# Attention scores from three products a tile, queries paired two steps ahead, one copy moved from ScalarE to GpSimd

## What is computed

```
Q = layernorm(x) @ Wq.T + bq      K = ctx @ Wk.T + bk      V = ctx @ Wv.T + bv
scores = Q K^T * SCALE / temperature        (per head: 32 terms a score)
x = x + softmax(scores) V @ Wo.T + bo
```

## Time and profile before

| what | value |
|---|---|
| median of three runs | 1847.13 us |
| profiled execution: its own time | 1846.3 us |
| profiled execution: span of core 0 | 1844.5 us |
| mean granted TensorE clock | 0.985 |
| `attend` in the profile | about 164 to 936 us |
| `rest` in the profile | from about 936 us |

### The profile page before, as it was taken

One profiled execution on the slowest core, in us unless ns is written; L12 is line 12 of the kernel. 1 busy time (PEld: TensorE's weight loads), 2 busy tenths in 40 slices (PEclk: granted clock), 3 DMA queues, 4 the chain that ended last, 5 costly groups with the idle time before them and its releaser, 6 DMA issues. The chain is left out here.

```text
span 1844.5 us, 30104 instructions
## 1 busy us (share of the span) xinstructions
PE 1766.0 (96%) x9338; PEld 1327.2 (72%) x9418; DVE 1562.1 (85%) x3587; ACT 1232.8 (67%) x3374; POOL 969.4 (53%) x1079
## 2 busy tenths in 40 slices
PE   8897799999999999999879999889999999999997
PEld 7676688888888888888744444357677777777775
DVE  6865889999999999988769888888888988888885
ACT  4574999999999999999733333265665655665543
POOL 2333466666666666666610000056776776676664
PEclk9998999999999999999989999999999999999999
DMA  8565334544454445433379999154455455454311
GB/s 303 194 225 151 81 103 119 133 122 115 118 133 122 115 116 135 119 94 92 81 227 380 401 396 390 74 206 157 162 173 176 160 172 180 155 173 162 129 58 40
DMA packets 143278, 306.35 MB, mean 166 GB/s; under 512 B 44432, under 2 KB 52624, under 8 KB 125456
## 3 DMA queue, kind: packets, MB, share of 16 engines
q1 hardware_dynamic: 142976, 304.17, 51.4%
q10 hardware_dynamic: 144, 0.26, 0.0%
HBM read 164.90 MB, written 105.91 MB: 147 GB/s over the span
## 5 line engine op out<-in xcount | busy, mean ns | idle before, releaser
L1261 POOL TENSOR_TENSOR a_pr<-a_pr,a_rcp 128x512 f32<-128x512 f32 x256 | 266.4, 1041 | 281.4 <-DVE a_rcp L1107 281.2
L1017 ACT ACTIVATE a_pr<-a_s,a_nmax 128x128 f32<-128x128 f32 x1024 | 364.0, 380 | 15.8 <-DVE a_nmax L1100 14.2
L1507 PE MATMUL f_pair<-f_room,w 128*128 128x512 bf16 x999 | 224.7, 382 | 2.6 <-ACT f_room L1618 1.3
L1017 ACT ACTIVATION_READ_ACCUMULATOR a_pr<-a_s,a_nmax 128x1 f32 x1024 | 224.0, 219 | 0.0
L1926 POOL TENSOR_TENSOR f_rs<-f_rs,f_half 128x1 f32<-128x1 f32 x128 | 121.2, 947 | 179.6 <-DVE f_rs L1773 179.6
L1727 DVE CUSTOM_DVE_ANT_0 f_hf<-f_pair,nb,sh 128x512 f32<-128x512 f32 x244 | 172.7, 748 | 29.4 <-PE f_pair L1507 29.2
L1100 DVE TENSOR_REDUCE a_nmax<-a_s 128x4 f32<-128x512 f32 x256 | 172.3, 673 | 15.4 <-PE a_s L907 15.2
L1656 ACT ACTIVATE f_room<-f_ring,f_off,f_rs 128x511 f32<-128x511 f32 (+1 forms) x128 | 104.4, 816 | 120.2 <-POOL f_off L1932 120.2
L1115 DVE TENSOR_TENSOR a_pTl<-a_pt,a_pTh 128x512 fp32r<-128x512 f32 x256 | 168.5, 679 | 19.1 <-ACT a_pTh L1029 18.5
L1507 PEld LDWEIGHTS f_pair<-f_room,w 128*128 128x128 bf16 x1024 | 99.5, 98 | 116.4 <-issue 3.2
L919 PE MATMUL a_pt<-ident,a_pr 128*128 128x128 f32 x1024 | 155.4, 274 | 3.9 <-POOL a_pr L1261 3.8
(11 more groups left out here) (381 smaller groups left out, 5071.5 us busy)
## 6 DMA issues: line engine op xcount, KB each, us to landing
hidden<-f_hf SPq DMA_DIRECT2D x57, 1024.0 KB, 8.5
f_hf<-hidden SPq DMA_DIRECT2D x57, 1024.0 KB, 4.8
xb<-x SPq DMA_DIRECT2D x16, 1024.0 KB, 5.7
ctxh<-bqreph SPq DMA_DIRECT2D x128, 128.0 KB, 2.3
ctxh<-bqrepl SPq DMA_DIRECT2D x128, 128.0 KB, 2.4
a_xr<-x SPq DMA_DIRECT2D x64, 256.0 KB, 3.8
x<-a_xr SPq DMA_DIRECT2D x64, 256.0 KB, 2.6
f_ring<-x SPq DMA_DIRECT2D x64, 256.0 KB, 3.2
```

Of the source, the lines that this page charges most:

```text
L1017: last = e.activation(pr[:, t, j, :], s_bank[t][:, j * P:j * P + P], ACT.Exp, bias=nmax[kk % 2][:, t, j:j + 1], accum_out=sums[kk % 2][:, ...
L1261: e.tensor_tensor(p, p, rcp[kk % 2][:, t, :].unsqueeze(2).to_broadcast([P, 4, KEYS]), ALU.mult).then_inc(*e_pn)
L1507: last = e.matmul(h_bank[(PAIRS * u + i) % 3][:, q, :], w1[:, k, f * P:f * P + P], xT[u % 2][:, k, :], start=k == 0, stop=k == KC - 1)
```

## The change

1. `scores`: a tile takes three products of 256 columns, not four. The 12 products of 32 rows that four heads need (three per head) are laid as blocks of 32 rows into three planes of 128 rows; plane 0 adds into columns 0 to 255, plane 2 into 256 to 511, plane 1 into 128 to 383.
2. Keys and queries are laid out for that: `KEY_BLOCKS` (six DMAs a quarter, as before) and `QUERY_BLOCKS` (eight DMAs a step, 384 rows of 512 values, where there were four with 256 rows). The keys of two of the four quarters of the first batch are loaded in `prepare`, those of the others in the first two steps of `attend`.
3. QUERY is 2, XT 6, LOAD 11: queries and all before them one step earlier. `paired` waits for the last scores of step kk, since it overwrites the tile they read. The order of TensorE, ScalarE and VectorE changes in step 0; from step 1 on it is as before, except that the first half of `queries` is behind `scores` 0 in steps 1 to 4 too.
4. `chi` leaves ScalarE. GpSimd's `clo` now first waits for `vsum`, copies `cs` to the high half and waits for its own copy.
5. `vals` takes three DMAs a quarter, not eight. GpSimd clears the values' tile with one memset, not four.

```diff
-KEY_ROWS = ((0, 0, 0), (0, 0, 64), (1, 1, 0))
+KEY_BLOCKS = ((0, 0, 0, 3, 0, 0), (1, 0, 1, 3, 0, P), (2, 1, 0, 2, 0, 0), (2, 0, 3, 1, 2, P), (3, 1, 2, 2, 1, P),
+              (3, 0, 0, 1, 0, 0))
+QUERY_BLOCKS = (((0, 0, 0, 64), (2, 0, 64, 64), (1, 64, 32, 64), (0, 64, 0, 32), (2, 96, 96, 32)),
+                ((1, 0, 32, 64), (0, 96, 0, 32), (2, 64, 96, 32)))
+KEYS_HERE = 2
...
-        LOAD, LN_A, LN_B, NORM, XT, QUERY = 10, 8, 7, 6, 5, 1
+        LOAD, LN_A, LN_B, NORM, XT, QUERY = 11, 9, 8, 7, 6, 2
...
                 e_exp.wait_ge(e, 4 * (u - 1) + (2, 1, 4, 3)[t])
-                for i in range(2):
-                    for n, x in enumerate(kt):
-                        last = e.matmul(s_bank[t][:, 256 * i:256 * i + 256], qs[kk % 2][:, i, t * P:t * P + P], x[:, c, i, :],
-                                        start=n == 0, stop=n == 1)
+                for plane, at in ((0, 0), (2, 2 * P), (1, P)):
+                    last = e.matmul(s_bank[t][:, at:at + 2 * P], qs[kk % 2][plane][:, t * P:t * P + P], kt[c][:, plane, :],
+                                    start=plane == 0, stop=plane == 1)
                 last.then_inc(*e_s)
...
-            def chi(b, kk):
-                o = kk - VALUE
-                if not there(b, o):
-                    return
-                u, c, g = b * TPB + o, o % 4, o // 4
-                e_vs.wait_ge(e, 2 * u + 1)
-                e.activation(cT[g % 2][0][:, c, :], cs[:], ACT.Copy).then_inc(*e_chi)
...
                 phi(b, kk, 2)
                 phi(b, kk, 3)
                 if opening:
-                    xhi(b, 0)
-                chi(b, kk)
+                    xhi(b, kk)
                 exp(b, kk, 3)
...
-            for c in range(KC):
-                last = e.memset(f32(vp[:, c, :, :]), 0.0)
-            last.then_inc(*e_const)
+            e.memset(f32(vp_room[:]), 0.0).then_inc(*e_const)
...
                 c, g = o % 4, o // 4
+                e_vs.wait_ge(e, 2 * (b * TPB + o) + 1)
+                e.tensor_copy(cT[g % 2][0][:, c, :], cs[:]).then_inc(*e_chi)
                 e_chi.wait_ge(e, b * TPB + o)
                 e.tensor_tensor(cT[g % 2][1][:, c, :], cs[:], f32(cT[g % 2][0][:, c, :]), ALU.subtract).then_inc(*e_clo)
...
-                if not there(b, o):
-                    return
+                if not there(b, o) or first(b) and o < ASKED:
+                    return
+
+                e_s.wait_ge(e, 4 * (b * TPB + o - 2) + 3)
                 for h, e_half in ((0, e_qhi), (1, e_qlo)):
-                    if not first(b) or o >= ASKED:
-                        e_half.wait_ge(e, b * TPB + o - ASKED)
-                    for i in range(2):
-                        e.dma_start(f32(qs[o % 2][64 * h:64 * h + 64, i, :]), f32(qT[h])[64 * i:64 * i + 64, :])\
+                    e_half.wait_ge(e, b * TPB + o - ASKED)
+                    for plane, to, at, n in QUERY_BLOCKS[h]:
+                        e.dma_start(f32(qs[o % 2][plane][to:to + n, :]), f32(qT[h])[at:at + n, :])\
                             .then_inc(e_qs[o % 2].sem, 16)
```

More of the change, by code:

```diff
@@ L819, in attend @@
         e_const, e_b = ev("const"), ev("bias", 16)
-        e_kt, e_v = ([ev(f"{n}{c}", unit) for c in range(KC)] for n, unit in (("keys", 96), ("values", 128)))
+        e_kt, e_v = ([ev(f"{n}{c}", unit) for c in range(KC)] for n, unit in (("keys", 96), ("values", 48)))
         e_qs = scr["e_qs"]
@@ L884, in xt @@
                     e_qlo.wait_ge(e, 1 - ASKED)
-                elif again:
-                    e_xlo.wait_ge(e, o - 1 - TURNED)
-                elif there(b, kk + QUERY):
+                elif there(b, kk + QUERY) and not (first(b) and kk < 0):
                     e_qlo.wait_ge(e, b * TPB + kk + QUERY - ASKED)
@@ L986, in step @@
                 pt(b, kk, 1)
-                if not opening:
+                if opening:
+                    xt(b, -1)
+                else:
                     queries(b, kk, 1)
                 scores(b, kk, 2)
+                if opening:
+                    queries(b, kk, 0)
+                    queries(b, kk, 1)
                 values(b, kk)
-                if opening:
-                    xt(b, -1)
                 pt(b, kk, 2)
@@ L995, in step @@
                 pt(b, kk, 3)
-                if not first(b) or kk >= 0:
-                    xt(b, kk, again=opening)
+                xt(b, kk)
                 out(b, kk)
@@ L1073, in step @@
                 if opening:
-                    xhi(b, -1)
-                elif not first(b) or kk > 0:
+                    qhi(b, kk)
+                else:
                     xhi(b, kk)
@@ L1212, in step @@
                 opening = first(b) and kk == 0
-                if opening:
+                if first(b) and kk < 0:
                     qlo(b, kk)
+                    return
                 rc(b, kk - 1, 3)
                 smax(b, kk, 0)
+                if opening:
+                    xlo(b, -2)
                 plo(b, kk, 0)
@@ L1220, in step @@
                 rc(b, kk, 0)
+                if opening:
+                    xlo(b, -1)
                 plo(b, kk, 1)
@@ L1227, in step @@
                 smax(b, kk, 2)
-                if not opening:
-                    qlo(b, kk)
+                qlo(b, kk)
                 vsum(b, kk, 0)
@@ L1232, in step @@
                 vsum(b, kk, 1)
-                if opening:
-                    xlo(b, -1)
-                elif not first(b) or kk > 0:
+                if not opening:
                     xlo(b, kk)
@@ L1381, in step @@
             def step(b, kk):
-                if not first(b) or kk >= 0:
-                    paired(b, kk)
+                paired(b, kk)
                 load(b, kk)
```

92 lines of the change are left out of this document (55 added, 37 removed).

## The result

| what | before | after |
|---|---|---|
| median of the runs | 1847.41 us | 1874.58 us |
| lowest and highest | 1845.5 to 1848.08 | 1874.15 to 1876.47 |
| ratio, 95% interval | | 1.0155 [1.0141, 1.0169] |
| span of the profiled execution | 1844.5 us | 1872.3 us |
| second `vlow` of step 0 and of step 63 | 189.56, 917.06 | 201.34, 946.41 |

`vlow` is ScalarE's reading of the attended values. The start of the second one of a step is called its zero. The change makes the kernel 1.55% slower, 27 us. The forecast was 1867 us (1855 to 1888) and slower with 0.86. The time lies in the range, 7.6 us above the forecast.

What follows compares the result with a forecast made beforehand. TensorE's queue was taken as the bound, by 0.25 us over the GpSimd loop. 57 x 11.89 + 6 x 10.85 = 742.8 against 727.5 us (+15.3), with 2.4 + 2 opening +19.7: 1866.0 profiled, 1867 us median, range 1855 to 1888.

Steps and rivals of the forecast that it cites:

- The loop: From zero over `xhi`, `xlo`, `rc` 2, `prob` 2, `clo`, `prob` 3, `pt` to next zero: 11.22 of 11.47 us, slack 0.25.
- What the prediction says of `rc` 3: In `attend`, VectorE's own queue holds `rc` 3, so ScalarE's saved 0.67 us is off the loop and worth nothing.
- The copy: In `clo` on GpSimd, between `prob` 2 and `prob` 3: 0.61 us plus 0.08 semaphore wait, 0.69 uncovered.
- The rival with a price of 1.04: GpSimd's copy costs 1.04 us like a two-input operation, adding 25 us: 1892 us; chance 0.10.
- The body by port speed: Copy on GpSimd at 1.03 cycles an element, 1.2 GHz: estimated 0.44 us for 512 elements, total 1857 us.
- Three products for four: In `scores`: four tiles save 0.48 us of TensorE's queue a step; the loop gains only one tile's 0.12.
- The step: Steady step of `attend`: loop 11.84 us, plus 0.05 for the step with normalisations, 11.89 us.
- The range of 1858 to 1876: The forecast's own range, from the opening's bounds and a copy on GpSimd between 0.525 and 0.75 us.
- The opening: Start of `attend`: four more SP loads, 2.4 us, plus step 0's full `queries` and `xt`, 2 us (bounds 0 and 4).
- SP's queue: Eight query issues take 4.8 us, `qhi` keeps 1.4 us slack; rival: SP late in 16 steps, 1883 us, chance 0.05.
- The last six steps and `rest`: Last six steps of `attend` have no `xt`: 10.85 us each; `rest` is untouched.
- nobody waits for those within a step: On SP behind `paired`, loads of x, store, reload, values and keys, some 11 issues, 6.6 us, hold nobody up.

Runs made afterwards that it cites:

- before_copy_pool: Kernel before with only the copy of the attended values' high half moved from ScalarE to GpSimd; 1868.95 us, ratio 1.0128.
- experiment 3: Changed kernel with the copy still on GpSimd, but copy and `clo` moved behind `prob` 3; 1853.1 us, ratio 1.0047.
- experiment 9: On experiment 6: step 0's queries behind `pt` slot 3, `clo` behind `prob` 3, `x1_stats` behind `rc` 3 and next `smax` 0; 1884.09 us, 1.0215.
- experiment 6: Also `stats_first`: changed kernel with the copy back on ScalarE and step 0's statistics and `rstd` ahead of all else in `attend`; 1838.9 us, 0.9967.
- experiment 7: Changed kernel, copy on GpSimd, with step 0's statistics and `rstd` ahead of all else in `attend`; 1864.3 us, ratio 1.0113.

## Why the prediction was right, and where it was off

**The loop: right, for more work in it.** "Nothing in between has slack", said of `xhi` to `prob` 3, and a slack of 0.25 us at `pt`, were what decided. In `before_copy_pool`, 0.69 us of new work on an engine with a third of its time idle cost 0.40 us a step, where 0.69 less 0.25 is 0.44. That is the step of the prediction that carries the sign, and the experiment that shows it changes nothing but the copy. What the prediction says of `rc` 3, that VectorE's queue holds it, is half of it: ScalarE's `exp` 3 ends 0.03 us ahead of it (506.38 and 506.41), so ScalarE's list was on this loop as much as GpSimd's. That didn't matter to the forecast, since the copy made GpSimd's way longer than the others (`prob` 3 ends at 7.45 us and not at 6.83). It is why less work on GpSimd gained nothing in experiments 3 and 9.

**The copy: right.** Forecast 0.61 with 0.08 for its own semaphore; measured 0.612 on average (0.609 to 0.619 over all 64), and 528.34 to 529.03 is 0.69. The rival with a price of 1.04 fell. The body by port speed that the prediction took from the Trainium skill, "GPSIMD Engine Reference", section 3.1 (an estimate of 0.44 us) is 0.17 too short for the instruction. But the growth from the cast of 128 columns to the one of 512 is 0.612 - 0.289 = 0.323 us for 384 columns, 0.84 ns a column, and 1.03 cycles at 1.2 GHz are 0.86. So the page's rule fits what each column adds, and what it leaves out is the fixed part, by an estimate from these two rows 0.18 us, with 0.08 for the wait behind it. The two casts differ in what they write (bf16 and fp32r), so this rests on the type making no difference, which no run here shows.

**Three products for four: right in its mechanism.** Forecast: four tiles save 0.48 us of TensorE's queue, one tile's 0.12 shortens the loop, and the rest is lost in the wait. Measured: 11.90 against 11.80 for the 0.12 (`before_copy_pool` and the changed kernel), and the idle time of 0.68 + 0.05 at `pt` for a forecast of 0.8. TensorE's busy share came out at 95.5% where "about 93%" was expected, since the view counts a product to its modelled end and not to the next one's start: 0.81 of 11.80 us is 7%.

**The step: right, and better than its parts.** 678.0 us in 57 steps are 11.89, the number of the prediction. A plain step of a window in the middle is 11.80 (forecast 11.84), one with the normalisations 11.96 to 12.02 (forecast 12.06). Steps 1 and 3 at 12.85 and 12.63, and one of 12.83 behind a late load of x, make up the difference. So a part of that agreement is chance. The range of 1858 to 1876 that the prediction calls its own would be 1860 to 1877 by the bounds that it names for it; the stated range of 1855 to 1888 doesn't hang on it.

**The opening: the term that was mis-sized.** The step of the prediction is "Step 0 now also holds a full `queries` and an `xt` (...) Bounds 0 and 4 us, I take 2." It measured 9.3, above the upper bound. SP's part, 4 x 0.6 = 2.4, was right: the eight issues take 5.0 us (160.79 to 165.80) where four took 2.5 (160.90 to 163.35). That the starts agree to the tenth is chance, since TensorE's first product lies between 165.96 and 167.37 in the ten profiles with eight loads, and at 164.07 and 164.94 in the two with four. For step 0 I had counted what TensorE gets more of. I had not asked which piece of the layer norm falls on it: with LN_B at 8 in place of 7, two more statistics and the `rstd` of the group land in step 0, where VectorE is late as it is and GpSimd's list puts `rstd` ahead of `prob` 2. Experiments 6 and 7 show that piece: 7.1 us, and without it 2.2 are left, which is about the 2 that I had for the rest. That the time still lies in the range is no merit of this term: the range was wide because of the copy's price. The row was not in the trace of before, but the lists were in the code.

**SP's queue: not the bound.** The eight issues take 5.0 us in most steps and up to 6.5 where 4.8 was forecast (5.9 in the step shown, from 524.64 to 530.58), and `qhi` never waits in the steady part.

**The last six steps and `rest`: small misses of either sign.** 67.1 us against 65.1: four of the six are 10.73 to 10.81, as forecast, and two are 12.30 and 11.63. And 1.5 less behind step 63, in code that the change doesn't touch: this part takes 924.6 to 926.5 us in the eleven other profiles, so it is the profile of before (927.4) that is long, and not the change that is short. No experiment took either up.

## What to carry to other kernels

Idle time of an engine is not room: follow one step through all engines, find the loop, and ask whether the idle time lies behind or ahead of the wait that the loop goes through. Here a third of GpSimd was idle, but a copy between `prob` 2 and `prob` 3 could use none of it; behind `prob` 3 most of its cost went. Then ask how many ways reach the point at which the loop closes. Here there were three within 0.1 us of each other, so a longer one cost at once and a shorter one gained nothing. When stages are moved one step earlier, write down what the first step holds on every engine's list, not only on the one whose work is moved.

A saving on the bound engine is worth only the slack of the next loop. Here 0.48 us of TensorE a step brought 0.23 because the loop over `prob` 3 was 0.25 us behind.

## What the runs showed that I had not expected

**A reload that is now sometimes late.** SP's reload of x for the output stands behind the query loads. In the kernel before it was issued 2.2 us after zero (503.09 and 500.88); with eight query loads it goes at 507.45, 7.2 us after the zero at 500.25, and GpSimd reads it in the next step. Landing takes 3.7 us by the median. It is not the landing that got worse: in the steady part of the kernel before it took up to 8.2 us, and nothing waited; here it takes up to 6.7. But GpSimd waits for it 12 times in the steady part, 21.7 us in all, in the row of `a_xr` above. The longest one was issued at 400.99:

```profile
400.99 0.43 SPq L1384 DMA_DIRECT2D a_xr<-x  x1
```

```profile
407.75 1.30 POOL L1287 TENSOR_TENSOR a_xr<-a_xr,a_bo 128x512 f32<-128x512 f32 x1 [3.53 <-DMA a_xr<-x]
```

GpSimd could start 6.8 us later, and the step was 12.83 us, 1.0 more than its neighbours. In `stats_first` one such wait was 5.1 us and its step 15.25, 4.0 more. This is the rival with SP's queue in another shape: not `qhi` was late but a load that the prediction had passed with "nobody waits for those within a step". Most of these waits cost nothing: of the steps in which they lie, two are longer than a plain one, the one of 12.83 and one of 12.05 us, 1.3 us together. So its price differs from one execution to the next. Issuing the reload ahead of the query loads was not tried.
